# A new order of the steps on all engines of a fused adaLN block: attention masks among transposes, other places for normalization, quantization and copies

## What is computed

```python
h = _layernorm(x, axis=-1) * (1 + ca) + sa
q, k, v = h @ Wq, h @ Wk, h @ Wv                 # 16 heads of 64
s = einsum('bhid,bhjd->bhij', q * scale, k)
p = where(causal_mask, 0.0, exp(s - max(s)))
out = (p @ v) / (sum(p) + 1e-8)
x = x + ga * (out @ Wo + bo)
h = _layernorm(x, axis=-1) * (1 + cb) + sb
gate, y = fp4_linear(h, w_gate), fp4_linear(h, w_up)
x = x + gb * fp4_linear(silu(gate) * y, w_down)
```

## Time and profile before

| | before |
|---|---|
| median of 3 runs | 1363.34 us (1361.21 to 1366.97) |
| profiled execution, its own time | 1361.84 us |
| its span | 1359.9 us |
| granted TensorE clock, mean | 0.988 |
| busy: PE, PEld | 1272.2 us (94%), 1032.7 us (76%) |
| busy: DVE, ACT, POOL | 1102.7 us (81%), 835.7 us (61%), 843.4 us (62%) |
| HBM traffic over the span | 19 GB/s |

### The profile page before, as it was taken

One profiled execution on the slowest core, in us unless ns is written; L12 is line 12 of the kernel. 1 busy time (PEld: TensorE's weight loads), 2 busy tenths in 40 slices (PEclk: granted clock), 3 DMA queues, 4 the chain that ended last, 5 costly groups with the idle time before them and its releaser, 6 DMA issues.

```text
span 1359.9 us, 34237 instructions
## 1 busy us (share of the span) xinstructions
PE 1272.2 (94%) x10194; PEld 1032.7 (76%) x10194; DVE 1102.7 (81%) x2565; ACT 835.7 (61%) x2885; POOL 843.4 (62%) x1582
## 2 busy tenths in 40 slices
PE   5999999999999999999999999999999999999973
PEld 3677887777887777787777787777788777788762
DVE  5678888888888888888888888888888888888775
ACT  3766666666666665666765665756666666666640
POOL 1656566766666666666666656576656676666563
PEclk9999999999999999999999999999999999999995
DMA  3000000000000000000000000000000000000000
GB/s 101 17 19 17 18 14 17 21 21 15 21 10 19 20 21 20 17 10 21 17 21 21 15 10 21 17 21 21 15 15 16 17 21 21 15 21 6 19 19 10
DMA packets 38056, 26.53 MB, mean 20 GB/s; under 512 B 2800, under 2 KB 33392, under 8 KB 38032
## 3 DMA queue, kind: packets, MB, share of 16 engines
q1 hardware_dynamic: 38032, 26.23, 6.7%
HBM read 21.94 MB, written 4.28 MB: 19 GB/s over the span
## 4 chain that ended last, share of the span: by engine, by line
POOL 50%; issue 33%; PE 9%; DVE 3%; ACT 2%; POOLq 2%; DMA 1%; SPq 0%; DVEq 0%; ACTq 0%
POOL probs L437 21%; POOL qy L75 6%; POOL qy L73 5%; POOL probs L435 4%; POOL hq L77 3%; PE ps_m L827 3%; POOL h2a L484 2%; POOL rstd L445 2%; PE ps_s L922 2%; POOL h L488 2%; PE ps_o L949 2%; PE ps_m L806 1%; POOL x_keep L479 1%; POOL x_gb L459 1%; POOL xq L77 1%
## 5 line engine op out<-in xcount | busy, mean ns | idle before, releaser
L563 ACT ACTIVATE probs<-ps_s,neg_max 128x128 f32<-128x128 f32 (+1 forms) x1024 | 425.7, 431 | 393.2 <-PE ps_s L931 393.2
L437 POOL TENSOR_SCALAR probs<-probs,r_den 128x256 f32<-128x256 f32 (+1 forms) x768 | 349.3, 472 | 0.0
L736 DVE TENSOR_REDUCE neg_max<-ps_s 128x4 f32<-128x1024 f32 x256 | 303.8, 1218 | 2.5 <-PE ps_s L922 2.1
L922 PE MATMUL ps_s<-qk 64*128 64x256 f32 x2048 | 260.0, 393 | 1.5 <-ACT probs L563 1.0
L435 POOL TENSOR_TENSOR probs<-probs,r_den 128x128 f32<-128x128 f32 x256 | 102.5, 400 | 238.4 <-DVE r_den L745 232.9
L662 DVE COPY probs_t<-ps_m 128x512 f32<-128x512 f32 x256 | 176.4, 689 | 90.7 <-PE ps_m L806 86.5
L806 PE MATMUL ps_m<-ident,probs 128*128 128x128 f32 x1536 | 230.4, 273 | 1.4 <-DVE probs_t L662 0.8
L922 PEld LDWEIGHTS ps_s<-qk 64*128 64x128 f32 x2048 | 186.1, 187 | 49.1 <-issue 12.4
L563 ACT ACTIVATION_READ_ACCUMULATOR probs<-ps_s,neg_max 128x1 f32 x1024 | 218.6, 213 | 0.0
L949 PE MATMUL ps_o<-probs_t,v 128*64 128x256 f32 (+1 forms) x2048 | 194.7, 332 | 1.6 <-ACT o_t L555 1.6
L73 POOL TENSOR_TENSOR qy<-qy,qm 128x352 f32<-128x352 f32 (+1 forms) x96 | 83.1, 865 | 180.4 <-DVE qm L66 178.6
(11 more groups left out here) (107 smaller groups left out, 1804.1 us busy)
## 6 DMA issues: line engine op xcount, KB each, us to landing
mod_a<-mod_rows SPq DMA_DIRECT2D x32, 256.0 KB, 3.3
x_in<-L_attn_x SPq DMA_DIRECT2D x32, 128.0 KB, 2.1
x_res<-L_attn_x SPq DMA_DIRECT2D x32, 128.0 KB, 2.1
out<-y_out SPq DMA_DIRECT2D x32, 128.0 KB, 1.8
mod_b<-mod_rows SPq DMA_DIRECT2D x32, 64.0 KB, 2.8
wkv<-L_attn_Wkv SPq DMA_DIRECT2D x2, 512.0 KB, 6.9
wq<-L_attn_Wq SPq DMA_DIRECT2D x1, 512.0 KB, 4.0
wo<-L_attn_Wo SPq DMA_DIRECT2D x1, 512.0 KB, 8.1
```

The source lines that it names most:

```text
L437: ins = nc.gpsimd.tensor_scalar(cols, cols, r_den[:, u % 4, s:s + 1], 1.0, ALU.mult, ALU.mult)
L563: ins = nc.scalar.activation(probs[:, u % 4, h, t * P:(1 + 2 * t) * P], ps_s[:, 2 * (u % 2) + h, t * N:t * N + (1 + t) * P], ACT.Exp, bias ...
L736: nc.vector.tensor_reduce(neg_max[:, u % 4, :], ps_s[:, 2 * (u % 2):2 * (u % 2) + 2, :].rearrange("p b (t j) -> p (b t) j", t=2), AX.X, AL ...
L922: mm = nc.tensor.matmul(ps_s[:, 2 * (u % 2) + h, t * N:(t + 1) * N], qk[rows, u % 4, 0, t * P:(t + 1) * P], qk[rows, u % 4, 1, :], start=( ...
```

## The change

No instruction is added or removed. The order changes on TensorE, ScalarE, VectorE and GpSimd; SyncE's stays. One wait is relaxed: `down` of half k asks for the transposes of that half only. The weight-placement step of the first bodies moves along with `gate`. In the same manner as below for ScalarE, VectorE's and TensorE's bodies are now written out stage by stage.

```diff
         SHARED = (
-            ("t0", "qk0", "t1", ("v", 0, 0), ("xqt", 2, 0), "qk1", "t2", ("gate", 2, 0), ("v", 0, 1)),
+            ("t0", "qk0", "t1", ("v", 0, 0), ("xqt", 2, 0), "qk1", "t2", ("v", 0, 1), ("gate", 2, 0)),
             ("t0", "qk0", "t1", ("up", 2, 0), ("gate", 2, 1), "t2", "qk1", ("up", 2, 1), ("wo", 1, 0), ("wo", 1, 1)),
-            ("t0", "qk0", "t1", ("v", 0, 2), ("hqt", 2, 0), "t2", "qk1", ("v", 0, 3), ("xt", -1, 0)),
-            ("t0", "qk0", "t1", ("hqt", 2, 1), "t2", "qk1", ("down", 2, 0), ("down", 2, 1)))
+            ("t0", "qk0", "t1", ("v", 0, 2), "t2", ("hqt", 2, 0), "qk1", ("v", 0, 3), ("xt", -1, 0)),
+            ("t0", "qk0", "t1", "t2", ("down", 2, 0), ("hqt", 2, 1), "qk1", ("down", 2, 1)))
...
-                    pe.wait_ge(hqt_ready, 2 * (b + 1))
+                    pe.wait_ge(hqt_ready, 2 * b + k + 1)
```

GpSimd (the order of before, by stage, was: 0: units -1, 0, keep. 1: unit 1, residual, input_rstd, round_hidden 0, unit 2. 2 and 3 as now):

```diff
+                    if j == 0:
+                        normalize(i, -1)
+                        normalize(i, 0)
+                        keep()
+                        residual()
+                    elif j == 1:
+                        input_rstd()
+                        normalize(i, 1)
+                        normalize(i, 2)
+                        round_hidden(i - 2, 0)
+                    elif j == 2:
+                        normalize(i, 3)
+                        attended_rstd()
+                        normalize(i, 4)
+                        modulate()
+                    elif j == 3:
+                        normalize(i, 5)
+                        round_hidden(i - 2, 1)
+                        normalize(i, 6)
+                        round_ffn_in()
```

ScalarE, where `shared_reads(n)` reads the step at place n of the stage's row of `SHARED` (nothing where another engine reads it):

```diff
+                    elif j == 2:
+                        exponentials(4, 0)
+                        exponentials(4, 1)
+                        shared_reads(1)
+                        exponentials(5, 0)
+                        shared_reads(3)
+                        shared_reads(4)
+                        shared_reads(5)
+                        exponentials(5, 1)
+                        shared_reads(6)
+                        shared_reads(7)
+                        shared_reads(8)
+                        out_copy()
+                    elif j == 3:
+                        exponentials(6, 0)
+                        exponentials(6, 1)
+                        shared_reads(1)
+                        exponentials(7, 0)
+                        shared_reads(3)
+                        shared_reads(5)
+                        out_copy()
+                        exponentials(7, 1)
+                        shared_reads(6)
```

VectorE, stages 1 and 3 (before, the input's statistics stood at the end of stage 0 ahead of the last gate read, its normalization at the end of the quantization of stage 1, and stage 3 read t1 before the scales):

```diff
+                    elif j == 1:
+                        input_stats()
+                        denominators(1)
+                        maxima(2)
+                        maxima(3)
+                        shared_reads(1, 0)
+                        input_normalized()
+                        shared_reads(1, 2)
+                        shared_reads(1, 3)
+                        shared_reads(1, 4)
+                        hidden_scales(i - 2, 0)
+                        hidden_magic(i - 2, 0)
+                        shared_reads(1, 7)
+                        shared_reads(1, 8)
+                        denominators(2)
+                        shared_reads(1, 9)
...
+                    elif j == 3:
+                        denominators(5)
+                        maxima(6)
+                        h_low_part()
+                        maxima(7)
+                        shared_reads(3, 0)
+                        ffn_in_scales()
+                        shared_reads(3, 2)
+                        denominators(6)
+                        shared_reads(3, 4)
+                        ffn_in_magic()
+                        shared_reads(3, 7)
```

More of the change, by code:

```diff
@@ L448, in body, with normalize, round_hidden, residual @@
                 has = Has(i)
-                for j in range(PAIRS):
-                    if has.unit(2 * j - 1):
-                        normalize(i, 2 * j - 1)
-                    if j == 1 and has.prev:
+                def normalize(b, u):
+                    if has.unit(u):
+                        normalize_unit(b, u)
+                def round_hidden(b, k):
+                    if has.prev2:
+                        round_hidden_half(b, k)
+                def residual():
+                    if has.prev:
                         pool.wait_ge(res_loaded, 16 * i)
@@ L552, in out_copy @@
                     def out_copy():
+                        if not has.unit(2 * (j - 2)):
+                            return
                         at = 2 * ((j - 2) % PAIRS)
@@ L557, in exponentials @@
                     def exponentials(u, h):
+                        if not has.attn:
+                            return
                         act.wait_ge(masked, 16 * i + 2 * u + h + 1)
@@ L723, in hidden_scales @@
                 def hidden_scales(b, k):
+                    if not has.prev2:
+                        return
                     dve.wait_ge(h_ready, 2 * b + k + 1)
@@ L740, in denominators @@
                 def denominators(u):
+                    if not has.unit(u):
+                        return
                     dve.wait_ge(exp_done, 16 * i + 2 * u + 2)
@@ L784, in body, with ffn_in_scales @@
-                    if j == 3 and has.prev:
+                def ffn_in_scales():
+                    if has.prev:
                         dve.wait_ge(h2_ready, i)
```

219 lines of the change are left out of this document (138 added, 81 removed).

## The result

| | before (measured again beside it) | after |
|---|---|---|
| median | 1362.67 us (4 runs) | 1328.19 us (1327.69 to 1328.81, 4 runs) |
| ratio | 1 | 0.974 [0.972, 0.977] |
| profiled execution, span | 1361.84, 1359.9 us | 1328.32, 1326.5 us |
| granted TensorE clock, mean | 0.988 | 0.988 |

The account below looks back on a forecast made before the run. TensorE was taken to bound the kernel, so only its waits could be won: period 40.50 to 40.2 us, 9.3 us over thirty periods, plus 2.8 in the last batches, from 1361.84 to 1350 us; range 1318 to 1369.

Parts of the forecast that it names:

- Floor: 40.50 - 1.43 - 0.57 = 38.50 us.: Steady period on TensorE without hqt1's wait (1.43) and the short waits for late-read PSUM banks (0.57).
- The sum of new waits: TensorE waits the new order adds per period, all four stages: 0.29 + 0.19 + 0.50 + 0.71 = 1.69 us.
- rival A: Larger gain: the charged ScalarE orders do not bind, exponentials run ahead of the replay; 1326 us, chance 0.25.
- hqt1's wait: Fourth stage: transposes of the second gated half wait for GpSimd's rounding; the reorder removes 1.43 us a period.
- Stage 1, t2's wait of 0.19: Second stage: VectorE normalizes the input before reading t1, so t2 waits 0.19 us.
- None of it on TensorE's path: costed at nothing: Input normalization moved to where GpSimd idles: 1.2 us off VectorE, but no gain for TensorE.
- Masks, 0 of 0 to 0.05 each: Eight masks a period now between other TensorE steps: extra cost bounded by 0 and 0.05 us each, taken as 0.
- Scales ahead of t1's read, 0.10: Fourth stage: VectorE's FFN-input scales precede its t1 read, which frees hqt1's bank; 0.10 us, bounds 0 and 0.5.
- The start "gain or lose up to 2: zero": First batches, where weight rounding now precedes normalization: up to 2 us either way, counted as zero.
- C: Slower: GpSimd's unit 3 normalization, behind unit 2 and the first half's rounding, holds up stage 2's t1; 1371 us, chance 0.12.
- D: VectorE's attended normalization under unit 4's GpSimd tensor_scalar stretches from 0.84 to 2.02 us, delaying maxima; 1368 us, chance 0.03.
- theory P: Expectation set for experiment 8: a late step costs its wait plus about 0.10 us; second stage 0.35 to 0.45 us less.

Follow-up runs that it names:

- Experiments 8: Kernel before with only ScalarE's second-stage order as in the change (tanh and attention-output copy ahead of unit 3's exponentials): 1357.2 us, ratio 0.996.
- experiment 9: Kernel before with the edits of experiments 1 and 8, and TensorE's second-stage masks placed as in the change: 1325.1 us, ratio 0.972.
- experiment 1: Kernel before with only the fourth stage's TensorE order (t2, down0, hqt1) and the relaxed wait of down: 1337.7 us, ratio 0.981.
- experiment 5: Changed kernel with GpSimd's old order in the first two stages and VectorE's input normalization back behind the quantization: 1352.2 us, ratio 0.993.
- experiment 10: Changed kernel, first batch's weight rounding behind GpSimd's first normalization, third stage's attention-output copy ahead of xt's copies: 1322.8 us, ratio 0.971.
- experiment 11: Kernel of experiment 10 with VectorE's scales of the feed-forward input behind its read of t1 in the fourth stage: 1317.1 us, ratio 0.967.
- experiment 12: Kernel of experiment 10 with ScalarE's copy of v ahead of unit 5's first exponential and of t2 ahead of unit 7's: 1324.3 us, ratio 0.971.
- experiment 2: Changed kernel with ScalarE's order of before, masks left in their new places: 1383.0 us, ratio 1.015.
- experiment 13: Kernel of experiment 12 with, in the first stage, v's copy ahead of unit 1's first exponential and qk1's ahead of the second: 1334.2 us, ratio 0.979.
- experiment 6: Changed kernel with only GpSimd's order of the first two stages put back (first half's rounding ahead of unit 2): 1342.8 us, ratio 0.986.

## Why the prediction was wrong

Against the steady period forecast, stage by stage:

| stage | floor + new waits, forecast | after | late starts in after | so the floor was |
|---|---|---|---|---|
| first | 9.05 + 0.29 | 9.37 | 0.54 | 8.83 |
| second | 12.02 + 0.19 | 11.72 | 0 | 11.72 |
| third | 8.77 + 0.50 | 9.06 | 0.45 | 8.61 |
| fourth | 8.66 + 0.71 | 9.20 | 0.83 | 8.37 |
| sum | 38.50 + 1.69 | 39.35 | 1.82 | 37.53 |

The late starts are the excess of each pitch between first matmuls over the shortest that the same step has: 0.22 + 0.06 (t2), 0.15 + 0.11 (gate) in the first stage; 0.06 + 0.06 (hqt0), 0.23 + 0.10 (qk1) in the third; 0.38 (values), 0.06 + 0.10 (down0), 0.19 + 0.10 (qk1) in the fourth. Where there are two numbers the second is the lost lead.

- **The step that failed: "Floor: 40.50 - 1.43 - 0.57 = 38.50 us."** The lengths of "unhindered steps" were taken where the step itself, or the one behind it, started late: down 0.87 (0.76 on time before scores), gate or up 0.60 (0.50 before another step), xqt 0.25 (0.18), wo 3.74 (3.66). They held the lost lead of a weight load, which isn't shown as idle and which the bracket on the matmul's row doesn't hold. The first down of the earlier trace rows was on time itself (its first two matmuls 0.110 apart, 0.213 in the second down), and its 0.87 hold 0.2 us in which the second waited for its bank. The floor was 0.97 us too high, 29 us over thirty periods. Experiments 8 and 9 show it: they bring the second stage to 11.92 and 11.70, under its "floor" of 12.02, without any instruction removed.
- **The sum of new waits was nearly right**: 1.69 forecast, 1.82 found. That is partly luck: only 1.29 of the 1.82 are waits and 0.53 are lost leads, which the prediction didn't know, and single waits were off by up to 0.2 us either way (gate 0.06, found 0.15; values 0.20, found 0.38; down0 0.33, found 0.06; qk1 in the fourth stage 0.08, found 0.19). In the first stage a floor 0.22 too high and late starts 0.25 too low cancel, 9.34 against 9.37. ScalarE's orders do bind, as charged: v's copy holds up qk1 in the third stage (11.4 us over the span) and t2 in the first (8.3 us), t2's copy holds up qk1 in the fourth (10.6 us). So rival A's time, 1326, came true by another way: its reason, that these waits would not bind, is wrong.
- **hqt1's wait**: gone, as forecast, and 1.23 of the 1.43 us show up in experiment 1's fourth stage.
- **Stage 1, t2's wait of 0.19**: did not come. It rested on the normalization taking 0.84 us ahead of the read of t1; alone it takes 0.60 (next section), and the read ends in time.
- **"None of it on TensorE's path: costed at nothing"** for the parting: right for the kernel before, as experiment 9 shows, and wrong for the change, where taking it back, with the two orders that made it, costs 0.8 us a period (experiment 5), in the third and fourth stages and not at the t2 that the prediction named.
- **Masks, 0 of 0 to 0.05 each**: the masks cost nothing themselves; their places are worth 0.19 us a period.
- **Scales ahead of t1's read, 0.10**: nothing in the change, since `values` and all behind it was 0.38 late anyway; 0.255 as soon as that cover went (experiments 10, 11). No slow tiny instruction was behind it, only the order.
- **The start "gain or lose up to 2: zero"**: 4.9 us lost, more than both bounds; weight rounding ahead of the probabilities is the likely half of it (2.4 us with both amendments of experiment 10, 0.9 in experiment 12). With ScalarE's old order batch 2 begins at 96.1 (experiment 2), so that order may have a part in it too; the two were not tried together, and the cause of this loss stays open. **The tail, 2.8**: 3.2.
- **C**: the chain is there and sits exactly where it was put; in the change it is in time. **D** did not happen: the attended normalization takes 0.83 as before, since the GpSimd instruction that holds it up is a short one (last section).

The sum with what was measured: 1361.84 - 35.2 + 4.9 - 3.2 = 1328.3.

Open: why theory P's 0.4 us of experiment 8 came only with the masks moved too. The trace shows where (up1 0.585 to 0.487, qk1 with its second half 0.86 to 0.79), and that ScalarE's copies there come earlier in relation to TensorE's steps; no run moved the masks of the second stage alone.

## What to carry to other kernels

Take a step's unhindered length from an occurrence whose first weight load begins ahead of its first matmul, and compare several; a late step hides up to 0.1 us inside its busy time, its length up to the next step's start can hold that one's wait too, and a floor built from late steps will call a gain impossible. Split a broad reordering before believing its stated reason: here two small pieces gave all of it, and the new places of GpSimd's and VectorE's work only kept on time what the rest of the change had made tight. Moving a read ahead on a busy reader can move the wait to the next step: of the three kernels that made such moves on ScalarE two were slower and one had as long a period as before, one stage shorter and one longer by the same 0.19 us. And look who releases a step again after each mend: GpSimd's rounding, gone as a releaser in the change, is back in experiments 9 and 11.

## What the runs showed of the hardware

VectorE's two normalization instructions, each with two SBUF inputs, take three lengths by what GpSimd does beside them. With GpSimd idle and under its tensor_scalar, both in the kernel after:

```profile
664.53 0.60 DVE L771 SCALAR_TENSOR_TENSOR xn<-x_in,mv,rstd 128x128 f32<-128x128 f32 x2
...
678.95 0.83 DVE L771 SCALAR_TENSOR_TENSOR xn<-x,mv,rstd 128x128 f32<-128x128 f32 x2
...
678.28 1.37 POOL L437 TENSOR_SCALAR probs<-probs,r_den 128x256 f32<-128x256 f32 x3
```

Under its tensor_tensor they take 2.02, each about as long as GpSimd's instruction. Taken one by one, VectorE's two of the second case and the first and third of GpSimd's three tell more:

```profile
678.95 0.35 DVE L771 SCALAR_TENSOR_TENSOR xn<-x,mv,rstd 128x128 f32<-128x128 f32 x1
...
679.22 0.56 DVE L771 SCALAR_TENSOR_TENSOR xn<-x,mv,rstd 128x128 f32<-128x128 f32 x1
...
678.28 0.48 POOL L437 TENSOR_SCALAR probs<-probs,r_den 128x256 f32<-128x256 f32 x1
...
679.08 0.57 POOL L437 TENSOR_SCALAR probs<-probs,r_den 128x256 f32<-128x256 f32 x1
```

VectorE's first takes 0.35, with GpSimd idle it takes 0.34. GpSimd's third, which began behind it, takes 0.57 where an equal one took 0.48. VectorE's second, which began behind that, ends 0.14 us after it. The kernel before shows the same distance under the tensor_tensor:

```profile
721.95 1.01 DVE L711 SCALAR_TENSOR_TENSOR xn<-x_in,mv,rstd 128x128 f32<-128x128 f32 x1
...
722.90 0.93 POOL L75 TENSOR_TENSOR qy<-qy,qm 128x352 f32<-128x352 f32 x1
```

VectorE's first ends at 722.96 and GpSimd's instruction beside it at 722.82; VectorE's second ends at 723.97 and GpSimd's at 723.83. So both cases look like one: VectorE's instruction is held until GpSimd's is nearly done, and the stretch is as long as what is left of GpSimd's.

The prediction called 0.84 "the full speed" and said that the trace did not agree with the Trainium skill ("SBUF — State Buffer", Who interferes with whom). That was wrong: the full speed is 0.60, and the trace agrees with the rule, the full block included. The stretch was only 0.24 us because little was left of GpSimd's short tensor_scalar. A tiny tensor_scalar of one input can be caught as well: 0.90 us instead of 0.16 (experiment 6), as in the earlier trace rows, where it ends at 1347.55 and GpSimd's tensor_tensor beside it at 1347.53.
